# Cross-attention stage: sums over the context woven with products of the output projection

## What is computed

```python
x = x + attn(layernorm(x))            # 16 heads of 64, weights 1/(eps + distance)^2, then W_out
x = x + xattn(layernorm(x), ctx)      # 16 heads of 16, softmax over 77 context rows, then Wo
x = x + moe(x)                        # rmsnorm, top 2 of 8 experts, silu(up) * gate, W3
# xattn, per head: softmax(q k^T / 4 + mask) v ; the 16 heads side by side, @ Wo.T + bo
```

## Time and profile before

| | |
|---|---|
| median of 3 runs | 1605.2 us (1605.04 to 1605.32) |
| the profiled execution | 1606.14 us |
| its span in the trace | 1604.3 us |
| TensorE busy with matmuls | 1440.8 us (90%) |
| VectorE, ScalarE, GpSimd busy | 1032.5, 928.5, 650.2 us |
| mean granted TensorE clock | 0.945 of full speed |

### The profile page before, as it was taken

How to read it: one execution, slowest core, us unless ns; L and a number is a source line. 1 busy time by engine, 2 the same in 40 slices (tenths; PEclk the granted TensorE clock), 3 DMA queues, 4 the chain that set the end, 5 groups by cost and what they waited for, 6 DMA issues and landing times. The chain is left out here.

```text
span 1604.3 us, 23093 instructions
## 1 busy us (share of the span) xinstructions
PE 1440.8 (90%) x7425; PEld 926.5 (58%) x7426; DVE 1032.5 (64%) x1359; ACT 928.5 (58%) x646; POOL 650.2 (41%) x484
## 2 busy tenths in 40 slices
PE   6899999999999999999997589988994799999996
PEld 4555555455545554555454277777773566666664
DVE  7888998889888888889887545555555411211211
ACT  1879888988898889888989312222221122222221
POOL 5255446544654465546542512121120233333331
PEclk9999999999999999999999788888885799999998
DMA  4000000000000000000000431111120034233312
GB/s 143 13 1 14 26 26 13 13 26 26 19 7 26 26 20 13 20 27 13 20 0 14 127 98 40 42 50 40 45 80 14 21 83 138 33 83 84 87 29 70
DMA packets 67484, 66.91 MB, mean 42 GB/s; under 512 B 5152, under 2 KB 59936, under 8 KB 67424
## 3 DMA queue, kind: packets, MB, share of 16 engines
q1 hardware_dynamic: 60160, 56.58, 10.9%
q0 software_dynamic: 7296, 9.97, 3.7%
HBM read 48.70 MB, written 19.92 MB: 43 GB/s over the span
## 5 line engine op out<-in xcount | busy, mean ns | idle before, releaser
L1613 POOL TENSOR_TENSOR v_aug<-v_aug,wts 128x1024 f32<-128x1024 f32 x96 | 254.3, 2649 | 249.2 <-ACT wts L1466 244.7
L984 DVE TENSOR_SCALAR wts<-ps_s,k 128x1024 f32<-128x1024 f32 x240 | 297.1, 1279 | 86.3 <-PE ps_s L537 66.0
L1458 ACT ACTIVATE wts<-wts 128x4096 f32<-128x4096 f32 (+1 forms) x80 | 231.8, 2935 | 88.0 <-DVE wts L984 66.8
L552 PE MATMUL ps_o<-wts,g_r 128*64 128x512 f32 x1024 | 252.5, 616 | 12.8 <-ACT wts L1466 12.6
L1464 ACT ACTIVATE wts<-wts,eps_d 128x4096 f32<-128x4096 f32 (+1 forms) x80 | 241.6, 3020 | 0.2
L1466 ACT ACTIVATE wts<-wts 128x4096 f32<-128x4096 f32 (+1 forms) x80 | 235.2, 2940 | 2.5
L1379 DVE TENSOR_TENSOR wts<-rinv,ps_s 128x352 f32<-128x352 f32 x76 | 39.6, 521 | 254.3 <-ACT rinv L1531 171.2
L779 PE MATMUL ps_s<-wts,qk 128*128 x608 | 198.5, 470 | 3.1 <-issue 2.2
L973 DVE TENSOR_TENSOR v_aug<-v_aug,wts 128x1024 f32<-128x1024 f32 x96 | 156.2, 1627 | 5.4 <-ACT wts L1466 5.1
L537 PE MATMUL ps_s<-q_hi,k_hi 64*128 64x512 f32 x512 | 115.8, 446 | 41.1 <-DVE wts L984 31.2
L779 PEld LDWEIGHTS ps_s<-wts,qk 128*128 128x128 f32 x608 | 110.7, 192 | 65.1 <-issue 17.5
(11 more groups left out here) (238 smaller groups left out, 2417.0 us busy)
## 6 DMA issues: line engine op xcount, KB each, us to landing
wts<-in_w SPq DMA_DIRECT2D x16, 704.0 KB, 5.4
h_t<-o_raw SPq DMA_DIRECT2D x16, 512.0 KB, 2.7
qk<-h_t SPq DMA_DIRECT2D x16, 512.0 KB, 4.1
wts<-in_w SPq DMA_DIRECT2D x8, 640.0 KB, 7.2
raw_qk<-in_w_in SPq DMA_DIRECT2D x32, 128.0 KB, 2.2
raw_vg<-in_w_in SPq DMA_DIRECT2D x32, 128.0 KB, 2.2
acc<-wts SPq DMA_DIRECT2D x17, 128.0 KB, 1.8
wts<-in_x SPq DMA_DIRECT2D x2, 1024.0 KB, 6.0
```

Source lines behind the costliest of these rows:

```text
L552: mm = pe.matmul(ps_o[r, t], v_pair[:, b, r], wts[:, h, b, t], start=b == 0, stop=b == SB - 1)
L984: dve.tensor_scalar(wts[:, h, b, :], ps_s[:, h, :], k2[:, 2 * b + h:2 * b + h + 1], 0.0, ALU.add, ALU.max).then_inc(S_.max_ok, 1)
L1458: act.activation(chunk(start, end), chunk(start, end), ACT.Sqrt).then_inc(S_.sqrt_ok, 1)
L1613: pool.tensor_tensor(acc_w[:, 0], acc_w[:, 0], wts[:, 0, b], ALU.add).then_inc(S_.add_ok, 1)
```

## The change

On TensorE, `attn_out` and `x_values` can now be called for part of their products, and `step` puts them in another order. All four `turn_p` calls and `turn_x` stand together; the eight products of `attn_out` are spread over the step, one by one or in twos; the 16 heads of `x_values` come in groups of 6, 6 and 4 with one product between groups. On VectorE, `copy_xt` moves behind `probs_t` 3, `copy_xq` behind `expert_in`, and `copy_gates` ahead of `residual`.

```diff
-            def attn_out(i, part, n):
-                if part == 0:
+            def attn_out(i, q0, q1, n):
+                if q0 == 0:
...
-                for q in range(part * H // 4, (part + 1) * H // 4):
+                for q in range(q0, q1):
                     mm = pe.matmul(bank_a[:, 0:D], h_tile[:, q, :], w_o[:, q, :], start=q == 0, stop=q == H // 2 - 1)
-                if part:
+                if q1 == H // 2:
                     mm.then_inc(S_.y_mm, 1)
...
-            def x_values(i, n):
-                if n >= 1:
-                    pe.wait_ge(S_.x2_ok, i)
-                pe.wait_ge(S_.pta_ok, 2 * i + 2)
-                pe.wait_ge(S_.ptd_ok, 2 * i + 2)
-                for h in range(XH):
+            def x_values(i, h0, h1, n):
+                if h0 == 0:
+                    if n >= 1:
+                        pe.wait_ge(S_.x2_ok, i)
+                    pe.wait_ge(S_.pta_ok, 2 * i + 2)
+                    pe.wait_ge(S_.ptd_ok, 2 * i + 2)
+                for h in range(h0, h1):
...
-                mm.then_inc(S_.avx_mm, 1)
+                if h1 == XH:
+                    mm.then_inc(S_.avx_mm, 1)
...
             def step(t, n, s1=True, s2=True, s3=True, s4=True):
                 if s3:
-                    turn_p(t - 2, 0, n - 2)
-                    turn_p(t - 2, 1, n - 2)
+                    for k in range(4):
+                        turn_p(t - 2, k, n - 2)
                 if s2:
                     turn_x(t - 1, n - 1)
-                if s3:
-                    turn_p(t - 2, 2, n - 2)
-                    turn_p(t - 2, 3, n - 2)
+                if s1:
+                    attn_out(t, 0, 1, n)
                 if s2:
                     query(t - 1)
+                if s1:
+                    attn_out(t, 1, 3, n)
+                if s2:
                     logits(t - 1, n - 1)
-                if s3:
-                    x_values(t - 2, n - 2)
-                if s1:
-                    attn_out(t, 0, n)
+                for h0, h1, q in ((0, 6, 3), (6, 12, 4), (12, XH, None)):
+                    if s3:
+                        x_values(t - 2, h0, h1, n - 2)
+                    if s1 and q is not None:
+                        attn_out(t, q, q + 1, n)
                 if s4:
                     turn_y(t - 3, s2)
+                if s1:
+                    attn_out(t, 5, 6, n)
                 if s3:
                     turn_o(t - 2)
                 if s1:
-                    attn_out(t, 1, n)
+                    attn_out(t, 6, 7, n)
                 if s4:
                     gates(t - 3)
+                if s1:
+                    attn_out(t, 7, 8, n)
                 if s3:
                     x_out(t - 2)
...
             def step(t, n, s1=True, s2=True, s3=True, s4=True):
                 if s3:
                     probs_t(t - 2, 1, n - 2)
-                if s2:
-                    copy_xt(t - 1)
                 if s4:
                     norm_x2(t - 3, n - 3)
                 if s3:
                     probs_t(t - 2, 3, n - 2)
                 if s2:
-                    copy_xq(t - 1)
+                    copy_xt(t - 1)
                 if s4:
                     expert_in(t - 3, n - 3)
+                if s2:
+                    copy_xq(t - 1)
...
                 if s3:
                     copy_o(t - 2)
+                if s4:
+                    copy_gates(t - 3)
                 if s1:
                     residual(t, n)
-                if s4:
-                    copy_gates(t - 3)
```

## The result

The changed kernel takes 1612.1 us, the median of 19 runs (1604.7 to 1616.4); the kernel before, 1605.2 in 19 runs beside them (1594.7 to 1607.5). The ratio is 1.0048 (95% interval 1.0034 to 1.0061): 7 us slower, where 9.4 were forecast. The profiled execution took 1615.7 us, 3.6 above that median. That is 2.7 more than the medians differ by, since the profiled execution of before lay only 0.9 above its own median.

A forecast was written before the change was run, and what follows sets the result against it. TensorE bounds the kernel, 26% of the loop at half clock. Step 16.6 + 2.65 = 19.25 us against 18.55: +8.4 over 12 steps, perhaps +1 before the loop, giving 1614.6 us; own range 1605 to 1626, 8 in 10 runs 1586 to 1626.

The forecast's parts named there:

- The waits at full clock: Loop step with the new order, no half clock: 16.6 us against 16.1, +0.5 a step, bounds 0 and +0.9.
- this wait, for the division: Ahead of the turn of o, TensorE waits for two VectorE steps after the sums, about 0.3 us.
- the load of the next tile end last: Ahead of a tile's first product: the load, hidden before, lands at +4.7 us, after the turns end at 4.3.
- The clock: Clock falls in the weave in three steps of four, 8.5 us each, costing 2.65 us a step against 2.45; bounds 0, 4.0.
- no dense stretch until `x_out` and the turns: After a fall in the sums, nothing dense enough follows to restore the clock, so each fall lasts 8.5 us.
- The sum: Whole kernel: loop +8.4 us, steps 2 and 3 before it perhaps +1, drain steps as before: 1614.6 us.
- rival 1: The weave holds the clock in the loop: 1582 us, or 1592 with one short fall in two steps; chance 0.25.
- The row at 963: Trace row before the change: 2.26 us of sums, then 1.04 of projection, nearly a third, and the clock still fell.
- Rival 3: The turns put together lose the clock too, slowing query, two products and most logits: +43 us, 1648; chance 0.05.
- the earlier trace: Trace before the change: at 1205.4 to 1208.7 x_out's end, then transposes ran at 0.50; the next window had full clock.

The follow-up runs named there:

- e4: Kernel before with six of the eight products woven into the sums, one ahead of and one behind the turn of o, turns as before: 1573.1 us, 0.9808.
- e12: Changed kernel with its new order in the loop only, steps 0 to 3 and 16 to 18 in the old order: 1608.7 us, 1.0032 of before.
- e1: Changed kernel with the turns apart again and most of VectorE's copies back in their old places, weave kept: 1605.4 us, 1.0002 of before.
- e3: Kernel before with one product after head 6 and one after head 12 of the sums, turns as before: 1600.6 us, 0.9988 of before.
- e8: e4 with one product between query and logits and five in the sums: 1570.8 us, 0.9790 of before.
- e10: As e8, but two products ahead of the logits and four in the sums: 1571.8 us, 0.9801 of before.
- e5: Changed kernel with product 0 moved behind query, so products 0 to 2 stand ahead of the logits: 1614.0 us, 1.0049 of before.
- e11: Order of e10 in the hardware loop only, order of e4 in steps 0 to 3: 1563.0 us, 0.9764 of before.
- e2: Kernel before with the turns together and VectorE's copies copy_xt and copy_xq in their new places, nothing woven: 1655.7 us, 1.0326 of before.
- e7: As e4, but four products in the sums, two ahead of the turn of o and two behind it: 1585.8 us, 0.9887 of before.
- e6: e4 with the turns together and VectorE's copies as in e2: 1617.7 us, 1.0088 of before.
- e9: Kernel before, order kept, with product 0 made six more times in the sums and thrown away: 1611.4 us, 1.0047 of before.

## Why the prediction was right, step by step

**The waits at full clock.** Forecast: 16.6 us a step against 16.1, +0.5. Measured: 16.74 (988.33 less 971.59) against 16.18 in e4, whose turns are those of before: +0.56. That is the first step of the loop. The second step of the same order passed whole at full clock in e12 and took 16.93 there, which makes the difference 0.7. Most places are the forecast ones: about 1 us ahead of turn 2 and 0.34 ahead of turn 3 for the copies (1.35 in all, where I had written 1.7), and about 0.3 each ahead of `query` and of the logits. About 0.3 more lies ahead of the turn of o: the product before it takes 0.70 from start to start (985.18 to 985.88 in the first step), where 0.43 is its length. The forecast had this wait, for the division. One place was wrong: I had the load of the next tile end last in every step, but the first product waits for it in four of twelve, for 1.4 us in all. Over twelve steps the difference is 6.7 to 9 us, more than the loop's whole loss. e1 shows the turns as a cause: with them apart a step without a fall is back at 16.1 us, and the loop is 9.3 us shorter, a part of which is 7 us less of half clock.

**The clock.** Forecast: 2.65 us a step, up from 2.45. Measured: 18.97 - 16.74 = 2.23, against 18.55 - 16.18 = 2.37 before; over the loop 1.7 us are saved, not lost. (With 16.93 for the full-clock step it is 2.04.) That the thin weave does not hold the clock was right, and e3 shows it by itself. Two sizes inside the term were off in opposite directions, and that they nearly cancel is luck. I had falls in three steps of four; there were 11 in 12 steps. I had each at 8.5 us; they last 61 / 11 = 5.6. The reasoning that failed is "no dense stretch until `x_out` and the turns": the clock returned at 1007.2, behind a window of turns, single products and gates (1003.90 to 1007.10). The order that I took for too thin to bring the clock back brought it back after each of the eleven falls, within 6.8 us.

**The sum.** The loop was to lose 8.4 us and lost 5.0; the filling was to lose 1 and lost 2.4; the draining steps were to stay and lost 1.8. So 9.4 came out near 9.6 because a loop priced 3.4 too high made up for the 3.2 missing elsewhere. That closeness is luck; and as e12 shows, another execution of the same order divides the parts otherwise. The stated range, 1605 to 1626, is also narrower than its own terms: waits of 0 to 0.9 and a clock cost of 2.1 to 3.4 us a step give 1602 to 1628. In the filling I had seen that the load of a tile ends last, and priced it as in the loop. But in the second step the load is issued behind the store of the last pair and nothing covers it. The cause is the products ahead of the logits, which hold back the long chain to the exponential: from the first product to the third step it is 20.8 to 24.4 us in the nine kernels with none ahead of them in the filling, 26.2 with one (e8), 27.0 with two (e10), and 27.6 to 28.4 with three (e5, the changed kernel, e1). e11 confirms it: with the products ahead of the logits in the loop only, it is 24.0. The first draining step has the turns together with no product to fill the waits, as e2 has: 0.82 and 0.16 between the turns, 0.89 ahead of `query` and 0.70 ahead of the logits. I had called it unchanged, and that was plainly wrong by the same reasoning that priced the loop. With the old order it takes 14.43 (e12) where the changed kernel has 16.03.

**The rivals.** The clock did not hold (rival 1), though it can: it did for 44 us from 956.0 to 1000.4 in the changed kernel, in steps of 15.7 and 16.7 us, before the falls set in. The row at 963, from which I judged the weave, pointed the right way, and e3, e7 and e4 show how it goes on. Rival 3, the turns losing the clock, did not happen in the changed kernel: each fall of its loop begins in or right behind the sums. Its price was not idle, however. In e2 and e6 the clock does fall behind the turns, once the products that the change puts ahead of and behind `query` are missing. With them the stretch held; e5, which takes the one ahead of `query` away, has two falls there again. The Trainium skill, page "TensorE: Matmul & The Clock Gate", section "Part 4: PE-mode transpose", has transposes not engage the full clock. The runs disagree. In the draining of the changed kernel TensorE ran 16 transposes from 1215.26 on, at half clock, and the clock was full again at 1218.8, as in the earlier trace rows:

```profile
1215.40:1218.80 3.40, 3.40 (x17) 2.91 (x15) 2.04 (x5) 1.60 (x5) 0.50 (x1) 0.50 0.00 0
1218.90:1222.10 3.20, 2.33 (x21) 2.25 (x21) 1.17 (x2) 0.76 (x4) 0.12 (x1) 1.00 0.24 82
```

And in e4 the 18 transposes of a step stand in a row, with a wait of 0.69 us among them, and the clock is 1.00 through the loop.

## What to carry to other kernels

Where TensorE shows as busy and still runs at half clock, look at what stands where the clock falls. In this kernel it was a stretch of 32 records of 17 columns, which the profile shows as fully busy. Wide products that had to be made anyway kept the clock full there, but only if enough of them stood in the stretch: two among the 32 records did next to nothing, four halved the half clock, six were worth 2% of the whole kernel. Treat the hardware loop and its filling steps apart, since a product pulled forward over a load that the loop hides stands bare in the first steps.

## What the hardware showed unexpectedly

- Work that is thrown away can be nearly free: in e9 2.6 us of matmuls a step cost 0.2, because they bought back the clock.
- In e2 the clock fell behind a stretch of short matmuls with waits of 0.5 to 1.0 us between them, TensorE being busy for 1.55 of the 3.2 us before the fall, with no wait longer than 1.00. The transposes alone do not do it: in e4 the same 18 transposes stand in two groups with one named wait of 0.69, and the clock stays at 1.00 through the loop. Whether the same waits between other matmuls would do it was not tried.
- The same four products in the sums lost the clock every second step in e7 and never in the loop of e10, where two more stand ahead of the logits. Whether these two or the other length of the step (15.3 us against 16.2) decides was not tried. The filling of e10, with the same weave, did lose it once.
- The stage begins at 905.6 us (e11) to 914.4 us (e9) in the traces, behind a self-attention whose program is the same in all kernels. So a single span tells no more than some 5 us, and the parts of it were compared here each by its own start and end.
- The time of a kernel whose clock falls seems to wander more: 1600.7 to 1609.1 over ten runs of e1, and 1572.2 to 1573.9 over four of e4. The runs are few, and e6, whose clock falls too, stayed within 1617.1 to 1619.7 over four.
